# The causal stage's planned order: preparation a step earlier, parts as own items, later fetches

## The reference, cut to what matters

```python
x = x + _L1_attn_ref(_layernorm(x, axis=-1), Wqkv_w, Wqkv_b, out_w, out_b, W_static, Lambda_raw, Gamma, ...)
# inside, with 16 heads of 8:
scores = einsum('bhid,bhjd->bhij', q, k) * scale
y_softmax = einsum('bhij,bhjd->bhid', softmax(scores + causal_mask), v)
state = retention * state + Gamma * (v_t[..., :, None] * k_t[..., None, :])   # per time step
y_t = einsum('bhij,bhj->bhi', W_static + state, q_t)
alpha = sigmoid(gelu(x @ gate_w1 + gate_b1) @ gate_w2 + gate_b2)
y = alpha * y_softmax + (1.0 - alpha) * y_stp
return y @ out_w + out_b
```

## Time and profile before

| | us |
|---|---|
| median of 3 runs | 1810.27 |
| lowest, highest | 1807.2, 1813.46 |
| profiled execution, its own time | 1810.67 |
| its span, first to last instruction | 1809.4 |
| PE, DVE, ACT, POOL busy | 1568.5, 1285.6, 1101.3, 698.2 |
| one batch of the causal stage (batch 1) | 150.2 |
| the same, batches 0, 2 and 3 | 164.3, 150.2, 121.0 |

### The profile page before, as it was taken

One profiled execution on the slowest core, in us unless ns is written; L12 is line 12 of the kernel. 1 busy time (PEld: TensorE's weight loads), 2 busy tenths in 40 slices (PEclk: granted clock), 3 DMA queues, 4 the chain that ended last, 5 costly groups with the idle time before them and its releaser, 6 DMA issues. The chain is left out here.

```text
span 1809.4 us, 45598 instructions
## 1 busy us (share of the span) xinstructions
PE 1568.5 (87%) x19728; PEld 1003.6 (55%) x19728; DVE 1285.6 (71%) x2035; ACT 1101.3 (61%) x1642; POOL 698.2 (39%) x500
## 2 busy tenths in 40 slices
PE   4577998999999999999977778878888888899999
PEld 2354666778777778777853323433433332566665
DVE  4665745876787687777768768778778886766564
ACT  3265667777777777786733577677677678433321
POOL 4112301544354255425531555556465555301100
PEclk8798998999999999999996989999999999999999
DMA  7864200000000000000142462164236222000000
GB/s 180 198 181 109 41 5 12 2 2 2 1 2 2 2 2 2 2 2 2 48 110 62 146 155 72 48 187 95 71 116 143 72 71 72 1 7 12 7 12 12
DMA packets 43357, 102.59 MB, mean 57 GB/s; under 512 B 3944, under 2 KB 12288, under 8 KB 41428
## 3 DMA queue, kind: packets, MB, share of 16 engines
q1 hardware_dynamic: 40244, 94.17, 20.2%
q10 hardware_dynamic: 2912, 5.51, 1.8%
HBM read 67.42 MB, written 31.46 MB: 55 GB/s over the span
## 5 line engine op out<-in xcount | busy, mean ns | idle before, releaser
L1450 DVE TENSOR_REDUCE arena<-ring 128x2 f32<-128x1024 f32 (+2 forms) x320 | 342.1, 1111 | 88.8 <-PE ring L1307 63.4
L1550 ACT ACTIVATE arena<-ring 128x1024 f32<-128x1024 f32 (+1 forms) x320 | 291.6, 938 | 129.2 <-PE ring L1336 90.2
L1357 PE MATMUL accs<-arena 128*9 128x512 f32 (+3 forms) x1536 | 174.3, 528 | 2.7 <-ACT arena L1550 2.6
L2514 POOL TENSOR_TENSOR arena<-arena 128x1280 f32<-128x1280 f32 x28 | 65.3, 2332 | 287.0 <-PE accs L2275 231.7
L1329 PE MATMUL ring<-arena 51*128 51x512 bf16 (+3 forms) x768 | 124.4, 342 | 46.6 <-DVE arena L1450 24.9
L1300 PE MATMUL ring<-arena 48*128 48x512 bf16 (+3 forms) x768 | 126.6, 342 | 41.9 <-DVE arena L1450 21.7
L2506 POOL TENSOR_TENSOR arena<-arena 128x512 f32<-128x512 f32 x112 | 141.4, 1292 | 3.0 <-DVE arena L2316 3.0
L292 POOL TENSOR_SCALAR xn<-x,moments,rstd 128x128 f32<-128x128 f32 x80 | 64.4, 814 | 198.2 <-DVE rstd L263 182.6
L2781 ACT ACTIVATE arena<-ring 128x512 f32<-128x512 f32 x80 | 47.8, 598 | 147.2 <-PE ring L2636 142.6
L2499 POOL TENSOR_TENSOR arena<-arena 128x1024 f32<-128x1024 f32 x32 | 86.2, 2694 | 108.2 <-DVE arena L2373 108.2
L2741 DVE TENSOR_TENSOR arena<-arena,ring 128x512 f32<-128x512 f32 x80 | 55.0, 688 | 87.8 <-PE ring L2638 74.2
(11 more groups left out here) (346 smaller groups left out, 4225.8 us busy)
## 6 DMA issues: line engine op xcount, KB each, us to landing
arena<-whole_k SPq DMA_DIRECT2D x32, 512.0 KB, 4.6
arena<-whole_q SPq DMA_DIRECT2D x32, 512.0 KB, 6.2
arena<-c_scratch_q SPq DMA_DIRECT2D x14, 384.0 KB, 10.2
arena<-c_scratch_k SPq DMA_DIRECT2D x14, 384.0 KB, 13.3
a_scratch_k<-arena SPq DMA_DIRECT2D x8, 512.0 KB
c_scratch_k<-arena SPq DMA_DIRECT2D x8, 512.0 KB, 3.8
arena<-a_scratch_q SPq DMA_DIRECT2D x9, 384.0 KB, 7.2
arena<-a_scratch_k SPq DMA_DIRECT2D x9, 384.0 KB, 9.5
```

The lines of the kernel that those rows point to most:

```text
L1357: mm = nc.tensor.matmul(acc[ci % 2][32 * h:32 * h + HD + 1, a - c * BANK:BANK], c_values[b % 2][:, j, r * HEADS // 2 + 2 * g + i, :], weig ...
L1450: nc.vector.tensor_reduce(dst, src, AX.X, ALU.max, negate=True).then_inc(c_max_taken.up(item), 1)
L1550: nc.scalar.activation(view(c_probs[wi % 4]), view(ps), ACT.Exp).then_inc(c_weights_made.up(item), 1)
```

## The change

The items of `prepare` up to the turns come a step or two earlier; the value products come ahead of q, k a step earlier; the high part of q and k becomes an item of its own, `high`, with the POOL subtraction at its place; the loads of the stacks come a step earlier; `S` stands behind three maxima instead of two; the fetch of row j+1 becomes an item three steps behind `kv` j (with it the load of the weights `d`); `less` comes two steps earlier, `beta` one later.

```diff
--- before.py
+++ after.py
@@ -971,6 +971,13 @@
                 nc.vector.tensor_tensor(c_parts[:, 2, :], c_rest[:, :], c_parts[:, 1, :], ALU.subtract).then_inc(
                     c_split_first.up((side, "low")), 1)
 
+        def act_high(b, side):
+            before = ("q", b) if side == "k" else ("k", b - 1)
+            if before[1] >= 0:
+                ac.wait_ge(c_scratch_there[before[0]], before[1])
+            ac.wait_ge(c_full_made, (side, b))
+            nc.scalar.activation(c_parts[:, 0, :], c_full[:, :], ACT.Copy).then_inc(c_split.up((side, b, "high")), 1)
+
         def causal_first_act(item, ps):
             s, kind = "c", item[0]
             if kind == "log":
@@ -996,10 +1003,10 @@
                     ac.wait_ge(*split_done(*before, "rest"))
                 nc.scalar.activation(c_full[:, :], ps[:, :], ACT.Identity, bias=bias, scale=scale).then_inc(
                     c_full_made.up((kind, b)), 1)
-                if before[1] >= 0:
-                    ac.wait_ge(c_scratch_there[before[0]], before[1])
-                ac.wait_ge(c_full_made, (kind, b))
-                nc.scalar.activation(c_parts[:, 0, :], c_full[:, :], ACT.Copy).then_inc(c_split.up((kind, b, "high")), 1)
+                if b == 0:
+                    act_high(b, kind)
+            elif kind == "high":
+                act_high(*item[1:])
             elif kind == "mid":
                 _, b, side = item
                 ac.wait_ge(*split_done(side, b, "rest"))
@@ -1042,11 +1049,12 @@
             first_loads = [("L", 0, side, g, g + 1) for g in range(2) for side in "qk"] + loads(0, 1)
 
             prepare = lambda b: {
-                2: [("stats", b, 0)], 3: [("stats", b, 1)], 4: [("stats", b, 2)], 5: [("stats", b, 3)], 6: [("log", b)],
-                7: [("root", b)], 10: [("turn", b, 0)], 12: [("turn", b, 1)], 13: [("q", b)], 14: [("v", b, 0)],
-                15: [("mid", b, "q")], 16: [("write", b, "q"), ("v", b, 1)], 17: [("k", b)], 18: [("gate1", b)],
-                19: [("mid", b, "k")], 20: [("write", b, "k")], 21: [("gate2", b), *loads(b, 0)],
-                22: [("gate exp", b)], 23: [("alpha", b), *loads(b, 1)]}
+                1: [("stats", b, 0)], 2: [("stats", b, 1)], 3: [("stats", b, 2)], 4: [("stats", b, 3)], 5: [("log", b)],
+                6: [("root", b)], 8: [("turn", b, 0)], 10: [("turn", b, 1)], 11: [("v", b, 0)], 12: [("q", b)],
+                13: [("high", b, "q")], 14: [("v", b, 1), ("mid", b, "q")], 15: [("write", b, "q")], 16: [("k", b)],
+                17: [("gate1", b)], 18: [("high", b, "k")], 19: [("mid", b, "k")],
+                20: [("write", b, "k"), *loads(b, 0)], 21: [("gate2", b)], 22: [("gate exp", b), *loads(b, 1)],
+                23: [("alpha", b)]}
             pairs = NT // 2
             finish = lambda b: [[("att", b, 0)], [("att", b, 1)]] + [
                 [("tp", b, p)] + ([("att", b, p + 2)] if p + 2 < pairs else []) for p in range(pairs + 1)]
@@ -1054,7 +1062,7 @@
             for u in range(1, len(units)):
                 rows = maxima(units[u])
                 if u > 1:
-                    rows.insert(2, ("S", *units[u - 1], 0))
+                    rows.insert(3, ("S", *units[u - 1], 0))
                 ahead += rows
             ahead.append(("S", *units[-1], 0))
 
@@ -1070,13 +1078,15 @@
                 for j in range(HD):
                     s = at + 6 * j
                     side[s + (j == 0)].append(("kv", b, j))
+                    if j + 1 < HD:
+                        side[s + 3].append(("fetch", b, j + 1))
                     side[s + 3 + (j == 0)].append(("scan", b, j))
                     more = j < HD - 1
                     side[s + 4 + more].append(("scale", b, j))
                     side[s + 5 + more].append(("read", b, j))
                 end = at + (GROUPS - 1) * len(KEY_STEPS)
-                side[end + 6].append(("less", b))
-                side[end + 8].append(("beta", b))
+                side[end + 4].append(("less", b))
+                side[end + 9].append(("beta", b))
                 side[end + 11].append(("gated", b))
                 if b + 1 < batches:
                     side[end + 9].append(("vT", b + 1))
@@ -1091,7 +1101,7 @@
                      "alpha": (0, (("D", 1.5),), 0),
                      "vT": (2.0, (("D", 1.3),), 1), "beta": (1.0, (("A", 1.0),), 1), "S": (0.6, (("A", 1.0),), 1),
                      "att": (1.0, (("D", 1.5),), 1), "tp": (1.0, (("A", 0.6), ("D", 0.6)), 1), "stats": (0, (("D", 1.15),), 0),
-                     "log": (0, (("A", 0.5),), 0), "root": (0, (("D", 1.0),), 0), "mid": (0, (("A", 1.1),), 0),
+                     "log": (0, (("A", 0.5),), 0), "root": (0, (("D", 1.0),), 0), "mid": (0, (("A", 1.1),), 0), "high": (0, (("A", 1.1),), 0),
                      "scan": (0, (("D", 2.3),), 0), "scale": (0, (("A", 1.2),), 0), "A": (0, (("A", 0.6),), 0)}
 
             def times(item):
@@ -1497,7 +1507,7 @@
                     ps = slot.get(item)
                     if kind == "next":
                         moe_act(item[1:], ps)
-                    elif kind in ("log", "turn", "q", "k", "mid"):
+                    elif kind in ("log", "turn", "q", "k", "high", "mid"):
                         causal_first_act(item, ps)
                     elif kind == "gate1":
                         b = item[1]
@@ -1628,9 +1638,9 @@
                                     shift_signal(b, g, part).up((b, g, part), 16), 16)
                     elif kind == "vT":
                         sp_fetch(item[1], 0)
-                    elif kind == "kv" and item[2] + 1 < HD:
-                        sp_fetch(item[1], item[2] + 1)
-                        if item[1:3] == (0, 2):
+                    elif kind == "fetch":
+                        sp_fetch(item[1], item[2])
+                        if item[1:3] == (0, 3):
                             sp_load("d")
 
             def pool_program():
@@ -1658,16 +1668,16 @@
                     elif kind == "turn" and item[2] == 0:
                         pool_norm_tiles(s, item[1], 1)
                         add_bias(item[1])
-                    elif kind in ("q", "k"):
-                        b = item[1]
-                        before = ("q", b) if kind == "k" else ("k", b - 1)
-                        gp.wait_ge(c_split, (kind, b, "high"))
-                        gp.wait_ge(c_full_made, (kind, b))
+                    elif kind == "high":
+                        _, b, side = item
+                        before = ("q", b) if side == "k" else ("k", b - 1)
+                        gp.wait_ge(c_split, (side, b, "high"))
+                        gp.wait_ge(c_full_made, (side, b))
                         gp.wait_ge(c_split, (*before, "mid"))
                         if b >= 2:
                             gp.wait_ge(c_mixed, (b - 2, pairs - 1))
                         nc.gpsimd.tensor_tensor(c_rest[:, :], c_full[:, :], c_parts[:, 0, :], ALU.subtract).then_inc(
-                            c_split_pool.up((kind, b, "rest")), 1)
+                            c_split_pool.up((side, b, "rest")), 1)
                     elif kind == "mid":
                         _, b, side = item
                         gp.wait_ge(c_split, (side, b, "mid"))
```

## The result

The change makes the kernel slower. Its median over five runs is 1827.9 us (1823.35 to 1836.2) against 1810.27 over five runs of before; the ratio is 1.010 with an interval of 1.007 to 1.013. The forecast was 1793, range 1781 to 1812.

What follows compares the result with a forecast made beforehand. No engine is full; waits between four engines sharing one order and three ring buffers set the batch. Terms -3.6 - 4.4 - 3.0 - 1.5 - 5.3 = -17.8 from 1810.67 give 1792.9, median 1792.5, stated 1793; range 1781 to 1812.

Steps and rivals of the forecast that it cites:

- Statistics and root a step earlier: Normalisation for the next batch: +0.9 and +0.8 us on DVE in batches 1 and 2, +0.8 in batch 0, POOL uncounted.
- Own items for high parts, k and Gelu a step earlier: Preparation of q and k: -3.5 us each in batches 1 and 2; batch 0 -4.4, PE's 6.05 us wait gone.
- The two waits of 1.76 and 1.66 us: PE before the second value product and a W product, steps 16 to 18 of batch 1; both to go, -1.8 and -1.7.
- half-speed rows: Two V rows at the lower clock, 0.84 us each, should return to full speed with the waits: -1.7 us.
- The ceiling: Low part of k ends 1.3 us later, leaving 2.8 of 4.1 us slack: at most 2.8 gained up to step 26.
- rival A: Low part of k too late, PE waits 4.1 us for the new stacks in three batches: 1822 us, chance 0.13.
- Fetches three steps later: Row fetches on SP's queue: counted 0, with up to 2 us a batch in the range.
- S one maximum later: Steps 28 and 40 of three batches: half of PE's 1.06 us wait for POOL goes, -3.0 us, bounds 0 and -6.
- Less and beta: Step 44 turns: -0.5 us each in batches 0 to 2 (-1.5), -5.3 in batch 3, whose 3.60 us wait goes.
- The prediction's own sign of error: Wrong if batch 1 is not 2 us shorter, or batch 3's wait before beta becomes one for another engine.
- B: Rival: DVE paces the batches elsewhere, so PE's savings before step 19 are waited away later: 1807 us, chance 0.18.
- C: Rival: POOL's low part of q holds the scan, 2.1 us in three batches, +6.3: 1799 us, chance 0.11.

Runs made afterwards that it cites:

- experiment 5: The changed kernel with statistics, log, root and turns back at their old steps; 1825.15 us, ratio 1.0064 to before, stage 595.5 us.
- experiment 12: The changed kernel with the next batch's root behind read(0) and kv(1) on POOL; 1823.99 us, ratio 1.0063 to before, stage 595.4 us.
- experiment 6: The changed kernel with the middle part of k in step 18, right behind its high part; 1819.28 us, ratio 1.0029 to before, stage 595.8 us.
- experiments 3: The changed kernel with the old steps of preparation and loads, high right behind q and k, fetches still late; 1817.94 us, ratio 1.0026, stage 587.8 us.
- experiment 8: The kernel before with S one maximum later, less and beta moved, high an own item right behind q and k; 1808.73 us, ratio 0.9973, stage 581.5 us.
- experiments 10: The changed kernel with old normalisation steps, middle part of k in step 18 and fetches back beside kv; 1834.4 us, ratio 1.0136, stage 605.2 us.
- experiment 7: The changed kernel with the normalisation at its old steps and the middle part of k in step 18; 1814.47 us, ratio 0.9999, stage 585.2 us.
- experiment 9: The kernel before with only S one maximum later (some 130 maxima moved too); 1820.82 us, ratio 1.004, stage 589.9 us.
- experiment 11: The kernel before with less and beta moved, high an own item, S one maximum later except in batch 3; 1806.87 us, ratio 0.9965, stage 576.8 us.
- experiment 4: The kernel before with only less two steps earlier and beta one later; 1809.76 us, ratio 0.9987, stage 586.2 us.

## Why the prediction was wrong, by its own steps

*Statistics and root a step earlier: +1.7, in batch 0 +0.8, and nothing on POOL. This step failed, in batch 0.* DVE's part was costed; POOL's was "I count nothing, and up to 1.6 us a batch". By experiment 5 the early normalisation costs 1.0 and 2.2 us in batches 1 and 2, near the forecast, but 6.8 in batch 0. There the tiles wait for the root at the head of POOL's list and hold read(0), kv(1) and the split of the maxima (PE 4.17 us); experiment 12 changes this alone, V product 7 comes 4.7 us earlier, and 3.2 are left at the end of the batch. Two smaller things come with it. PE waits 1.04 and 0.45 us for the second set of tiles. And operations of POOL now meet the scans. Timelines of DVE and POOL of after, batch 1:

```profile
1175.86 2.28 DVE L1470 TENSOR_TENSOR_SCAN arena<-arena 128x1024 f32<-128x1024 f32 x1
...
1195.46 3.71 DVE L1470 TENSOR_TENSOR_SCAN arena<-arena 128x1024 f32<-128x1024 f32 x1
```

```profile
1174.15 5.20 POOL L292 TENSOR_SCALAR xn<-x,moments,rstd 128x128 f32<-128x128 f32 x4
...
1194.90 2.13 POOL L1685 TENSOR_TENSOR arena<-arena 128x1024 bf16<-128x1024 f32 x1 [1.17 <-ACT arena L1013]
```

Four tiles take 5.20 us with a scan beside them, 3.12 without. The later scan takes 3.71 us: the low part of q ran when it began and had 1.57 us to go, and 1.57 + 2.28 = 3.85. In experiment 5 the scans are back at 73.7 us. In experiment 12 they aren't, and it still gains 9.8, so the order of the list costs by itself. But it gains 3.2 to 3.4 us in each of batches 0 to 2, and experiment 5 mostly in batch 0; how the 9.7 us divide between order and such meetings no run here settles.

*Own items for high parts, k and Gelu a step earlier: -3.5, batch 0 -4.4. This held in batch 0 and failed in batches 1 and 2.* In batch 0 the wait of 6.05 us is gone. Experiment 5, without the early normalisation, is 7.7 us ahead of before at V product 18, where both have done the same products of the preparation. In batches 1 and 2 it is only 1.3 and 2.5 ahead. The two waits of 1.76 and 1.66 us became two of 1.79 and 1.49, both for ACT, in the same six steps (after keeps the one of 1.49). And the half-speed rows didn't come back: from V product 12 to 18 of batch 1 PE stands 6.8 us at the lower level in before, 7.4 in after. ACT's wait before the middle part of q was forecast as 1.1 to 1.6 us and is 1.10:

```profile
1193.77 1.06 ACT L1013 ACTIVATE arena<-arena 128x1024 bf16<-128x1024 f32 x1 [1.10 <-POOL arena L1679]
```

*The ceiling and rival A.* The low part of k was to end 77.5 us after the start of the batch (1210.1 in the prediction); it ended after 79.2 (1223.55), in before after 76.2. The high part ended 67.8 us after the start, ahead of the 69.0 from which rival A was to decide, and PE doesn't wait for the stacks in batch 1 of after (in batch 0 it does, 1.81 us). So A's wait of 4.1 us in three batches is wrong for the kernel as it is; its cause, the low part of k behind read and kv on POOL, is right and costs 9.4 us (experiment 6). It came out through a door that the ceiling didn't watch: the product on the fetched row.

*Fetches three steps later, counted 0. This step failed.* The prediction placed fetch(4) behind the fourth load, as it came, and held its product to have time until step 24, and its scan until step 27. The landing takes 10.6 us instead of 4.7, kv(4) waits 3.67, the scan 1.69, PE 2.56, and with the clock at 0.50 step 28 loses 3.3 us in batch 1 (6.3 in batch 0); with the low part early it loses 0.9 and 1.0 there (experiment 6). That experiment moves only the low part and is worth 9.4 us. With the old preparation the late fetch costs 6.3 us of the stage (experiments 3 and 8). Yet it is not bad by itself: with an early low part it is worth 20 us (605.2 against 585.2, experiments 10 and 7), since the writes of k then have no waiting fetch ahead of them.

*S one maximum later: -3.0.* Not borne out: the kernel of experiment 9 is 4.2 us longer. The prediction counted only PE's wait. It didn't see that in batch 3 the turn moves ahead of a V product, nor that the planner deals the maxima anew. What S costs by itself stays open.

*Less and beta: -1.5 and -5.3.* The waits went as said, in after too: from V product 43 to 44 it gains 2.1 us in batches 0 to 2 and 6.1 in batch 3. But 2.2 us come back in batch 3 by its end, with PE waiting 1.67 for ACT before the last V product, and S had taken 3.5 at step 28. Where S stays as before in that batch (experiment 11) it is 2.9 us shorter, half of what was forecast: 6.0 ahead of before at V product 44, and 3.2 given back behind it. The prediction's own sign of error, a wait that only becomes one for another engine, came true in part.

*The sum.* The forecast was -17.8, with +4.2 for statistics and root in it, so its gains were -22.0. Experiment 7 has the change without its two costs, and its stage is 0.5 us shorter than that of before. So of the 37.3 us between forecast and measured stage, 15.8 are costs that were too small in the sum (20.0 instead of 4.2), and 21.5 are gains that didn't come. These are estimates, and the gains in experiment 7 stand against losses that nothing here takes apart, above all 1.3, 0.5 and 2.8 us from V product 28 to 43 of batches 0 to 2, with the clock.

*Rivals B and C.* C forecast +6.3 us on the scans in three batches, from the low part of q; the scans are 6.3 us longer (80.1 against 73.8). That the numbers agree is luck: scan(2) takes 3.71 us and not over 4, and the rest is another scan of batch 0 (4.33 us, beside the bias on POOL) and one of batch 3 (3.05, beside `less`). It is busy time, too, and not path. B's idea, that the batch is paced elsewhere, fits experiment 4 only. None of the rivals put two of these together: 1822 for A was the nearest.

*The clock.* I counted only half-speed rows that vanish (-1.7 a batch). In after batch 1 stands about 35 us at 1.2 GHz instead of 15. Over the kernels a longer stage mostly has more of it: stage 576.8 with 72 us at the lower level (experiment 11), 585.2 with 94 (7), 605.2 with 118 (after). But it is no strict rule: before has 70 us and 585.7, and experiment 8 has 87 and 581.5. Nor does it say what is cause and what is effect. A wait costs its length and what PE then does at half rate; in after that is 9.10 us of work in the stretch shown, which at full rate would be about half of it (an estimate from the two levels).

## What to carry to other kernels

When a step is moved in an in-order queue, list for each engine what it now stands ahead of, and price the wait of those that were pushed back, DMA queue included; here two such pushes on POOL cost 9.7 and 9.4 us, and neither was an added instruction. The worse one was a step whose own input was late: it stood at the head of the list and held steps that were ready. A DMA issued behind others is not free: take its landing time from the loads ahead of it. Where a planner deals other work around the moved step, compare the whole lists, or the edit isn't the one in the diff. Then ask of each forecast gain which wait ends last once this one is gone; here two waits for ACT only changed place. And test parts in pairs, for the same fetch edit costs 6.3 us with one neighbour and saves 20 with another.

## What the runs showed of the hardware that was not expected

A scan of two SBUF inputs and an operation of POOL exclude each other in both directions: a scan took 3.71 us instead of 2.28, four tiles 5.20 instead of 3.12. It shows in the length of the instruction and not in a wait, so the views of waits don't name it; the mean of the group does (2502 ns against 2307). The Trainium skill's rule (SBUF — State Buffer, Who interferes with whom), that the later one blocks fully, fits the scan, which began 0.56 us behind the low part of q. It doesn't fit the recorded starts of the tiles. Of the four it is this one that is long, and it began 0.16 us ahead of the scan, which kept its 2.28 us:

```profile
1175.70 2.88 POOL L292 TENSOR_SCALAR xn<-x,moments,rstd 128x128 f32<-128x128 f32 x1
```

In batch 0 an addition on POOL began 0.18 us ahead of a scan and kept its 2.35, and the scan took 4.33. So recorded starts less than 0.2 us apart don't tell who waits.

A fetch of 512 KB issued behind four loads of 384 KB landed after 10.6 us, against a median of 4.7; it landed 2.0 us behind the last of them.

The granted clock stood at 0.50 for 10.2 us around the end of a PE wait of 2.56 us. Earlier in the same batch it did so around one of 1.49 us, which ended at 1208.53, after two waits of 0.45 and 0.44 us:

```profile
1208.10:1218.30 10.20, 9.30 (x56) 2.33 (x58) 6.12 (x7) 6.34 (x7) 5.93 (x3) 0.50 0.24 89
```

Why such small waits bring a fall as long as the larger one stays open.
